# Beginning of the expert stage: first block's choice beside its dense products, weights turned over four PSUM banks by two engines, and only the needed loads in front

## The reference, cut to what matters

```
def _L0_ffn_ref(hidden_states, Wg, bg, Wu, bu, Wd, bd, Wq, keys, down_embed, up_embed):
    q = (hidden_states @ Wq).reshape(b, t, 2, H, RET // 2)          # H = 4, RET // 2 = 64
    sim = jnp.einsum('btphn,hkpn->pbthk', q, keys)                   # 64 keys on each side p
    sc, ix = jax.lax.top_k(sim, KPH)                                 # KPH = 8
    all_sc = (sx[..., :, None] + sy[..., None, :]).reshape(b, t, H, KPH * KPH)
    scores, pk = jax.lax.top_k(all_sc, KPH)                          # 8 of 1024 experts, per head
    w = jnp.einsum('btd,bthkd->bthk', hidden_states, de)             # de = down_embed[idx]
    w = jax.nn.silu(w) * jax.nn.softmax(scores, axis=-1)
    experts_states = jnp.einsum('bthk,bthkd->btd', w, ue)            # ue = up_embed[idx]
    mlp = jax.nn.silu(hidden_states @ Wg + bg) * (hidden_states @ Wu + bu) @ Wd + bd
    return mlp + experts_states
x = x + _L0_ffn_ref(_layernorm(x, axis=-1), ...)
```

## Time and profile before

| | before |
|---|---|
| time, median of 3 runs | 4814.46 us (4812.48 to 4838.97) |
| the profiled execution's own time | 4825.74 us |
| its span, first to last instruction | 4824.0 us |
| busy: PE / DVE / ACT / POOL | 91% / 62% / 54% / 28% |
| granted TensorE clock over the span | 0.949 |

### The profile page before, as it was taken

The page is one execution under the profiler, slowest core; times in us unless marked ns, Lnnn a source line. Parts: engine busy times, 40 slices in busy tenths (PEclk is TensorE's granted clock), DMA queues, the critical chain, the costliest instruction groups (busy, mean ns, idle before and its releaser), DMA issues. The chain is left out here.

```text
span 4824.0 us, 65303 instructions
## 1 busy us (share of the span) xinstructions
PE 4390.4 (91%) x23444; PEld 2343.9 (49%) x23444; DVE 2969.4 (62%) x5876; ACT 2601.5 (54%) x3092; POOL 1369.3 (28%) x1045
## 2 busy tenths in 40 slices
PE   4999999999996799999999988888789999999999
PEld 2544444444443465656556555555434444444443
DVE  5666676676653776767667645555456565655553
ACT  1444554554562454544444422222278888888888
POOL 2011111111111452434334310000044545454544
PEclk8788998998997899999999999999899999999999
DMA  7223333332301000000000000000176666666664
GB/s 181 55 54 94 68 82 80 81 73 63 94 16 50 0 1 1 1 1 1 1 1 1 1 14 1 1 0 0 26 162 160 149 160 147 154 149 155 153 151 99
DMA packets 145957, 322.78 MB, mean 67 GB/s; under 512 B 39504, under 2 KB 64480, under 8 KB 129264
## 3 DMA queue, kind: packets, MB, share of 16 engines
q1 hardware_dynamic: 137664, 310.88, 28.0%
q10 hardware_dynamic: 7920, 7.87, 0.5%
q0 software_dynamic: 64, 0.05, 0.0%
HBM read 237.93 MB, written 80.74 MB: 66 GB/s over the span
## 5 line engine op out<-in xcount | busy, mean ns | idle before, releaser
L1793 ACT ACTIVATE gelu_out<-hidden,b_col 128x1024 f32<-128x1024 f32 x1024 | 1085.3, 1111 | 170.1 <-PE hidden L1707 169.1
L532 ACT ACTIVATE probsT<-scoresT 128x1024 f32<-128x1024 f32 (+3 forms) x768 | 601.3, 810 | 523.5 <-PE scoresT L470 519.2
L580 DVE TENSOR_REDUCE maxima<-front 128x1 f32<-128x512 f32 (+3 forms) x1280 | 732.1, 631 | 202.9 <-PE front L442 138.6
L1773 POOL TENSOR_TENSOR combined<-combined,gated 128x512 f32<-128x512 f32 x480 | 615.1, 1281 | 676.6 <-DVE gated L1891 676.6
L948 POOL TENSOR_TENSOR pair_sums<-sims 128x1024 f32<-128x1024 f32 x256 | 481.5, 1902 | 831.6 <-DVEq L1065 510.7
L1707 PE MATMUL hidden<-slice_stack,w_stack 128*128 128x512 f32 x2048 | 626.1, 428 | 14.1 <-ACT gelu_out L1793 14.1
L1891 DVE SCALAR_TENSOR_TENSOR gated<-expert_out,b_col,gates_spread 128x512 f32<-128x512 f32 x480 | 359.4, 749 | 452.2 <-PE expert_out L1717 247.0
L1717 PE MATMUL expert_out<-gelu_out,w_sb 128*32 128x512 f32 x4096 | 547.1, 606 | 30.9 <-DVE gated L1891 26.1
L436 PE MATMUL front<-k_stack,q_stack 62*128 62x512 f32 (+3 forms) x1536 | 503.8, 448 | 75.0 <-DVE maxima L580 47.1
L1707 PEld LDWEIGHTS hidden<-slice_stack,w_stack 128*128 128x128 f32 x2048 | 352.7, 189 | 368.3 <-ACT gelu_out L1793 278.6
L382 POOL TENSOR_SCALAR_AFFINE_SELECT probsT<-probsT 128x512 f32<-128x512 f32 x256 | 164.4, 642 | 1250.4 <-ACT probsT L532 1250.4
(11 more groups left out here) (187 smaller groups left out, 6054.7 us busy)
## 6 DMA issues: line engine op xcount, KB each, us to landing
gates_spread<-gate_scratch SPq DMA_DIRECT2D x512, 256.0 KB, 4.9
stack_scratch<-split_parts SPq DMA_DIRECT2D x192, 256.0 KB, 3.1
slice_stack<-slice_scratch SPq DMA_DIRECT2D x128, 256.0 KB, 7.9
q_stack<-stack_scratch SPq DMA_DIRECT2D x64, 384.0 KB, 6.3
k_stack<-stack_scratch SPq DMA_DIRECT2D x64, 384.0 KB, 9.1
slice_scratch<-slice_parts SPq DMA_DIRECT2D x32, 512.0 KB, 6.4
x_tiles<-in_L_attn_x SPq DMA_DIRECT2D x8, 1024.0 KB, 11.8
out_x<-x_tiles ACTq DMA_DIRECT2D x15, 512.0 KB, 4.9
```

Of the source, the lines that this page charges most:

```text
L532: nc.scalar.activation(PT[:, i % NPT, 2 * pr:2 * pr + 2, at:BANK], ST[pr][:, :, at:BANK], ACT.Exp, scale=SCALE).then_inc(probs_ready, 1)
L580: nc.vector.tensor_reduce(dst, F[k % 3][:, 0:parts * w].rearrange("p (a k) -> p a k", a=parts), AX.X, ALU.max)\
L1773: nc.gpsimd.tensor_tensor(CM[:, par, hc, :], CM[:, par, hc, :], Y[:, u % 2, :], ALU.add)\
L1793: nc.scalar.activation(GH[:, k % 4, :, :], HP[k % HPB][:, :, :], ACT.Gelu, bias=b1c[:, u % E:u % E + 1])\
```

## The change

`expert_weights` fills four banks in turn (with room for four fills in flight); fills with an even number are copied by DVE, odd ones by ACT; `down` is turned before `sim_weights` is made, and SP issues the loads of `moves` in this block instead of in the one before. The biases come in one load each. In the main block, the wait for `weights_in` moves behind the front. ACT takes the Silus of block 0 in groups between its exponentials, DVE the `hidden` of block 0 between the heads of its choice. `norm(2, 0)`, `norm(2, 1)` come right behind `less_max(0)`, and `weigh` for tile 0 of block 0 right behind its choice.

```diff
@@ expert_weights @@
+        PS = [ctx.enter_context(nc.psum_tensor(f"prep{i}", [P, BANK], F32)) for i in range(4)]
+            @block.sync
+            def _(sp):
+                later_loads(sp)
             @block.tensor
             def _(pe):
+                def bank(n):
+                    if n >= 4:
+                        pe.wait_ge(copied_act if n % 2 else copied_dve, (n - 4) // 2 + 1)
+                    return PS[n % 4]
                 pe.wait_ge(loaded, 16 * (DC + 3))
...
+                for b in range(NB):
+                    ps = bank(n)
+                    for c in range(DC):
+                        mm = nc.tensor.transpose(ps[:, c * P:(c + 1) * P],
+                                                 DN[:, b, c * P:(c + 1) * P], ident[:, :])
+                    mm.then_inc(filled, 1)
+                    n += 1
                 for c in range(DC):
-                    wait(pe, copied, n)
+                    ps = bank(n)
...
             @block.vector
             def _(dve):
+                for n in range(0, 2 * NP + NB + DC, 2):
                     dve.wait_ge(filled, n + 1)
...
+            @block.scalar
+            def _(act):
+                act.wait_ge(zeroed, 1)
+                for n in range(1, 2 * NP + NB + DC, 2):
+                    act.wait_ge(filled, n + 1)
...
+                        op = nc.scalar.activation(MT[:, n - 2 * NP - NB, :], ps[:, :], ACT.Copy)
+                    op.then_inc(copied_act, 1)
@@ expert_ffn, loads @@
             sp.dma_start(DN[:, :, :], down.rearrange("(b p) d -> p b d", p=P)).then_inc(prep_in, 16)
-            for dst, src in moves:
-                sp.dma_start(dst, src).then_inc(weights_in, 16)
-        moves = [(UP[:, :, :], up.rearrange("(b p) d -> p b d", p=P)),
+        moves = [(bgc[:, :], bg.rearrange("(b p) -> p b", p=P)),
+                 (buc[:, :], bu.rearrange("(b p) -> p b", p=P)),
                  (wg[:, :, :], Wg.rearrange("(c p) f -> p c f", p=P)),
                  (wu[:, :, :], Wu.rearrange("(c p) f -> p c f", p=P)),
                  (wd[:, :, :], Wd.rearrange("(b p) d -> p b d", p=P)),
+                 (UP[:, :, :], up.rearrange("(b p) d -> p b d", p=P)),
                  (bdr[:, :], bd.rearrange("(a d) -> a d", a=1).to_broadcast([P, D]))]
-        for b in range(FB):
-            moves.append((bgc[:, b:b + 1], bg[b * P:(b + 1) * P].rearrange("(p a) -> p a", a=1)))
-            moves.append((buc[:, b:b + 1], bu[b * P:(b + 1) * P].rearrange("(p a) -> p a", a=1)))
+        def later_loads(sp):
+            for dst, src in moves:
+                sp.dma_start(dst, src, allow_slow_non_contiguous=True).then_inc(weights_in, 16)
@@ main block @@
+        SILUS_AFTER = {3: range(0, 4), 5: range(4, NB)}
+        SILUS_AFTER.update({8 + f: range(NB + f, NB + f + 2) for f in range(0, FB, 2)})
+        HIDDEN_AFTER = {8 + f: range(f, f + 2) for f in range(0, FB, 2)}
...
             for k in range(4 * TT):
                 copy_front(R[k % 2], k // (2 * TT), k // TT % 2, k % TT)
-            silus(0)
-            for t in range(TT):
-                exps(0, t)
+            act.wait_ge(weights_in, ALL_IN)
+            exp_top(0)
+            for k in range(TT * H):
+                exp_pairs(0, k // H, k % H)
+                for n in SILUS_AFTER.get(k, ()):
+                    silu(0, n)
...
             less_max(0)
-            for f in range(FB):
-                hidden(0, f)
+            for t in range(2):
+                norm(2, t)
+            dve.wait_ge(weights_in, ALL_IN)
             top_sum(0)
-            for t in range(TT):
-                choose(0, t)
+            for k in range(TT * H):
+                choose_head(0, k // H, k % H)
+                for f in HIDDEN_AFTER.get(k, ()):
+                    hidden(0, f)
             rest_to_last(0)
+            for a in range(2):
+                weigh(0, 0, a)
             for t in range(TT):
                 top_sims(1, t)
...
             less_max(1)
-            norm(2, 0)
-            norm(2, 1)
             second_half(0)
```

More of the change, by code:

```diff
@@ L958, in _ @@
             pair_sums(0)
+            pool.wait_ge(weights_in, ALL_IN)
             for m in range(NM):
@@ L978, in copy_front, with silu @@
                     nc.scalar.activation(SM[:, m % 2, t, :, :, :], bank[:, :], ACT.Copy).then_inc(front_free, 1)
+            def silu(m, n):
+                act.wait_ge(dg_done, ND * m + n + 1)
+                if n < NB:
+                    nc.scalar.activation(SD[:, n, :], R[n % 4][:, :], ACT.Silu).then_inc(dg_free, 1)
+                else:
+                    f = n - NB
+                    wait(act, h_done, FB * m + f - 1)
+                    nc.scalar.activation(GS[:, f % 2, :], R[f % 2][:, :], ACT.Silu, bias=bgc[:, f:f + 1])\
+                       .then_inc(dg_free, 1)
@@ L980, in silus @@
             def silus(m):
                 for n in range(ND):
-                    act.wait_ge(dg_done, ND * m + n + 1)
-                    if n < NB:
-                        nc.scalar.activation(SD[:, n, :], R[n % 4][:, :], ACT.Silu).then_inc(dg_free, 1)
-                    else:
-                        f = n - NB
-                        wait(act, h_done, FB * m + f - 1)
-                        nc.scalar.activation(GS[:, f % 2, :], R[f % 2][:, :], ACT.Silu, bias=bgc[:, f:f + 1])\
-                           .then_inc(dg_free, 1)
+                    silu(m, n)
@@ new lines, in exp_pairs @@
+            def exp_pairs(m, t, h):
+                T = TT * m + t
+                act.wait_ge(a_ready, H * T + h + 1)
+                if h < 2:
+                    wait(act, summed, 3 * (T - 1) + h + 2)
+                elif h == 2:
+                    act.wait_ge(s_begun, T + 1)
+                else:
+                    act.wait_ge(summed, 3 * T + 1)
+                nc.scalar.activation(E[h % 2][:, :], A[:, h, :], ACT.Exp, bias=NMX[:, H * t + h:H * t + h + 1])\
+                   .then_inc(e_ready, 1)
+                if h == 1:
+                    act.wait_ge(masked, H * T + 1)
+                    act.wait_ge(rz_ready, m + 1)
+                    wait(act, st_done, 2 * (TT * (m - 1) + t + 1))
+                    nc.scalar.activation(S[:, t, :], E[0][:, :], ACT.Copy, scale=RZ[:, H * t:H * t + 1])\
+                       .then_inc(s_begun, 1)
```

124 lines of the change are left out of this document (58 added, 66 removed).

## The result

The changed kernel takes **4790.55 us**, median of nine runs (4780.15 to 4807.64), beside 4830.27 for the kernel before (nine runs, 4812.48 to 4846.36): a ratio of 0.9921, 95% interval 0.9898 to 0.9945, which is 38 us less, with 27 and 49 as the ends (the two medians are 39.7 apart). The forecast was 4771, with a range of 4757 to 4799, and a gain of 43.5. The median missed it by 19.6, of which 15.8 are the kernel before, whose nine runs have a median that much above the three that the forecast started from; the other 3.8 are gain that did not come, within the interval of the ratio. The profiled execution of the changed kernel has an own time of 4790.55, a span of 4788.8 and a mean granted clock of 0.951 (before 0.949). PE's busy share went from 91% to 92%, which says little; what counts is when things happen behind the opening of the stage.

What follows compares the result with a forecast made beforehand. PE idling at the stage's opening, behind SP's loads, in the preparation and 38.05 us for chosen weights, was taken as the bound; 20.9 + 21.3 + 1.7 = 43.9, say 43.5, off 4814.46 gave 4771 us, range 4757 to 4799.

Steps and rivals of the forecast that it cites:

- Loads: Step 1, stage opening: PE waits only for `down`, no longer for SP's whole list, and starts 12.7 us earlier.
- the rival of a blocked queue: SP's queue: bias loads delay the 4 MB of weights until 1549, giving a slower kernel at 4829 us; chance 0.03.
- Preparation: Step 2, weight preparation: four banks and two engines keep PE going, 11.5 us against 15.6; the clock's rise saves 3.0 more.
- After 4 us at the half clock, 6.4 us of PE work are left: Preparation: PE's clock rises after 4 us, so the remaining work takes 3.2 us at full clock, saving 3.0 us.
- the front then begins warm: Main block's front: it starts at the full clock instead of running its first 4 us at half speed, gaining 1.1 us.
- steps 1 and 2: Loads and preparation, with the clock and the front: together they bring the main block's front 20.9 us forward.
- The rival that denied the rise: Preparation: the clock stays at half, costing 3.0 + 1.1 us, for a gain of 39.4 and 4775 us; chance 0.20.
- Choice beside the dense products: Step 3, block 0: grouped Silus and PE's products run beside the choice, bringing the chosen weights' signal 21.3 us forward.
- second price for a switch: Rival, ACT in block 0's choice: each table switch costs another 1.28 us, losing 15.4, for 4787 us; chance 0.03.
- The rival of the half clock inside the choice: Block 0's choice: PE falls to the half clock, products take 3.44 us, gain 17, 4797 us; chance 0.10.
- Order behind it: Step 4, block 0's signal to block 1's choice: 12.5 us instead of 14.2, gaining 1.7, with PE's 1.94 us turning uncovered.
- Passed on in full: Behind the start of block 1's choice: later blocks and stages are untouched, so the opening's gain is kept whole, once.

Runs made afterwards that it cites:

- e5b: Changed kernel plus ten unused identity products on PE before its wait for the loads; first load to block 1's first dense product 143.88 us (changed kernel 146.92).
- e8b: Changed kernel with `down` on its own semaphore, PE starting without it and turning it last; first load to block 1's first dense product 146.20 us.
- e2: Changed kernel with the old loads and old preparation, only the choice's new order left; first load to block 1's first dense product 165.70 us.
- e6: Changed kernel with identity products replacing the transposes of Wq and `down`; first load to block 1's first dense product 149.73 us.
- f1: e5b with SP's last three loads (Wd, up, bd) moved into the main block; first load to block 1's first dense product 142.81 us.
- e9b: Changed kernel with block 0's first `weigh` put back behind the tops of block 1; first load to block 1's first dense product 142.65 us.
- f4: Changed kernel unaltered, profiled and timed again; first load to block 1's first dense product 146.94 us, whole time 4792.79 us (0.9918 of the kernel before).
- f2: Changed kernel with `down` awaited separately and turned last, two identity products ahead, last three loads in main block, tile 0's `weigh` late; 4787.0 us (0.9907 of before).
- e7b: Changed kernel with `norm(2, 0)` and `norm(2, 1)` moved behind the sixth head of block 0's choice; first load to block 1's first dense product 146.70 us.
- f3: f2 with `norm(2, 0)` and `norm(2, 1)` moved behind the sixth head of block 0's choice; 4780.89 us (0.9888 of the kernel before).
- e1: Kernel before with only the later loads moved into the preparation's block; first load to block 1's first dense product 176.78 us (kernel before 188.54).
- e3: Changed kernel with the old preparation (two banks, DVE alone), new loads kept; first load to block 1's first dense product 153.46 us.

## Why the prediction was right, and the step that was off

**Loads.** 12.4 for 12.7: `down` was the last landing, 6.3 us behind its issue instead of the 5.9 taken over. SP's list ended at 15.6 behind the first load (15.4 by the forecast) and lay inside the preparation, by 2.8 us. It does so because the preparation ends late: in e5b and e8b, where it ends sooner, SP is what ends the block. The bias loads landed in 4.6 us and held the queue for 0.37 and 0.88 us, so the rival of a blocked queue had no ground.

**Preparation.** Four banks and two engines came out as worked: transposes 6.3 us for 6.2, no bank waited for. The step that failed is the clock's, as the prediction put it: "After 4 us at the half clock, 6.4 us of PE work are left" (3.0 us saved) and "the front then begins warm" (1.1). The clock rose 8.3 us behind the first record, which saved 1.3 (the products end at 1479.1; at the half rate of the earlier trace rows they would at 1480.4, an estimate), and was down again in the front's turns, which gained nothing. That is 2.9 of the 3.2 us by which steps 1 and 2 fell short. The term was taken from two rises elsewhere in the trace and from the reading that PE's stops at every pair of banks had kept the clock down in the old preparation. The second part does not hold: in e2 the clock rose inside that same preparation. And before the rise at 1496 PE had already worked for 15 us. The rival that denied the rise (0.20) was nearer in this term (2.9 of its 4.1), though not in its cause: e6 speaks against the transposes. That a warm front is worth about what the forecast said is shown by e5b, f1 and e9b, whose fronts took 1.3 to 1.4 us less; whether an execution gets it is not in the changed kernel's hands, since e9b got it with the same code and f4 did not. Why the rise comes when it does stays open.

**Choice beside the dense products.** 22.2 for 21.3, with each piece in its place: the norms 3.95 us beside POOL's sums, PE's wait with full banks 5.35 (5.8 forecast), 13 table loads of 1.28, no second price for a switch. The Trainium skill, "ScalarE: Activation LUTs", What ACT_TABLE_LOAD costs, adds a drain of about 1.38 us to each; by it, an estimate, some 16 us of gain would have been missing. The trace does not show the drain: the Silu starts 0.01 us behind its load. The rival of the half clock inside the choice happened for 6.8 us (1508.9 to 1515.8) and then ended, as PE worked without stopping. No price of it is to be seen here, since ACT never waited for PE in the choice: nine profiles with the changed kernel's order of the choice have 56.5 to 56.7 us from tops to turned weights. Only f2, with the same order, has 57.8, a price of some 1.2 to 1.4 us, and in e7b it was 1.7 (56.4 beside f3's 54.7).

**Order behind it.** 1.9 for 1.7. Rightly sized, but e9b shows that it is two things: taking the norms out of DVE's way brings 3.9 (14.1 to 10.2), the early `weigh` gives 2.0 back. The prediction had seen its uncovered wait and not asked what the opposite order would give.

**Passed on in full.** From the first mask of block 1 to its dense products 38.8 before and 39.0 after, and 3180.4 and 3180.6 behind that: the shift goes through to the end.

The whole gain came out within 2.3 us of the sum on the ruler because the one term that failed was small beside the waits that the change removed. That the median came out 19.6 off and still inside the range is mostly the starting point, which three runs had put 15.8 us too low.

## What to carry to other kernels

When a long stage-to-stage kernel is changed at one place, measure from an event ahead of the edit to one behind it, in more than one profile. Here that repeated to 0.03 us in the changed kernel and f4, where whole runs of it spread over 47, but e9b shows 2.2 us of difference in code that no edit had touched. A block ends with its slowest engine, so a list of loads, whose last issue held its queue for 5.3 to 6.7 us here, must be looked at again each time another engine of the block gets faster. Work in front of a wait (the early `weigh`) is only free where the wait has something to cover it.

## What was not expected of the hardware

- The clock's rise came 8.3 and 8.5 us behind the first record for transposes and for products, but 7.1 in e9b with the changed kernel's code, 5.9 when ten products filled the time before the loads landed, and 8.5 to 9.5 when none or two did (e8b, f2, f3). Behind PE's wait of 38.05 us in the kernel before it came after 4.4 us.
- Its fall: to 0.50 within 3.4 us of a rise in several kernels (changed, e1, e2, e3), with a pause of PE of 1.26 to 1.42 us at the block boundary, and no fall with a pause of 1.42 in e9b and of 2.58 in e5b. The length of the pause alone does not decide.
- The last load of the list, `bd`, held SP's queue for 5.3 to 6.7 us right behind the 1 MB loads, but 1.8 to 2.0 when it was issued later, with `Wg` and `Wu` landed and only `Wd` and `up` under way (f1, f2, f3).
- Two norms of 128x256 on DVE took 3.95 us beside POOL's first sums, 1.93 in e7b's place beside later ones, and 0.73 with POOL idle. That POOL is the cause was not tested by an edit.
- The attention ahead of the stage, identical code, took 1470.7 us to the first load in e1 and 1436.4 in e2, at mean granted clocks of 0.88 and 0.91. Windows of e1 and of e2:

```profile
38.00:1470.00 1432.00, 1328.33 (x9376) 669.93 (x9376) 916.71 (x1772) 706.70 (x999) 164.29 (x256) 0.88 0.32 73
```
```profile
38.00:1436.00 1398.00, 1288.88 (x9376) 654.37 (x9376) 916.30 (x1773) 705.53 (x999) 164.43 (x256) 0.91 0.32 75
```

PE has the same 9376 records and 39.5 us more of busy time in e1, DVE and ACT differ by about 1: the difference is PE's, with the lower clock, and it is the size of the whole gain.
